# A fused attention and expert block: start of the attention reordered, expert stage begun inside the attention's end

## The reference

```python
mod = (silu(c) @ wmod).reshape(4, 6, 1, 256)
sa, ca, ga, sb, cb, gb = (mod[:, n] for n in range(6))
ga, gb = (2 * (g >= 0) - 1) * max(abs(g), 0.25)      # for both
h = layernorm(x) * (1 + ca) + sa
x = x + ga * attention(h)      # 16 heads of 128, scores masked, softmax, W_O
h = layernorm(x) * (1 + cb) + sb
x = x + gb * ffn(h)
```

## Time and profile before

| what | us |
|---|---|
| median of three runs | 830.65 (829.01 to 832.02) |
| the profiled execution, its own time | 829.57 |
| its span, first to last instruction | 827.8 |
| TensorE busy | 796.7 (96%) |
| VectorE busy | 675.7 (82%) |
| ScalarE busy | 629.1 (76%) |
| POOL busy | 448.9 (54%) |
| mean granted clock of TensorE | 0.988 of 2.4 GHz |

### The profile page before, as it was taken

The page is one execution under the profiler, slowest core; times in us unless marked ns, Lnnn a source line. Parts: engine busy times, 40 slices in busy tenths (PEclk is TensorE's granted clock), DMA queues, the critical chain, the costliest instruction groups (busy, mean ns, idle before and its releaser), DMA issues.

```text
span 827.8 us, 14504 instructions
## 1 busy us (share of the span) xinstructions
PE 796.7 (96%) x4832; PEld 708.6 (86%) x4832; DVE 675.7 (82%) x1636; ACT 629.1 (76%) x1408; POOL 448.9 (54%) x310
## 2 busy tenths in 40 slices
...
DMA packets 47593, 70.54 MB, mean 85 GB/s; under 512 B 5536, under 2 KB 38464, under 8 KB 47392
## 3 DMA queue, kind: packets, MB, share of 16 engines
...
q10 hardware_dynamic: 144, 0.00, 0.0%
HBM read 25.49 MB, written 2.17 MB: 33 GB/s over the span
## 4 chain that ended last, share of the span: by engine, by line
PE 74%; ACT 11%; DVE 8%; issue 3%; POOL 2%; DMA 1%; SPq 0%; DVEq 0%; POOLq 0%; ACTq 0%
PE M L712 15%; PE M L713 15%; PE M L711 15%; PE S L711 6%; PE S L713 6%; PE S L712 6%; ACT PB L610 3%; PE T L711 2%; PE T L713 2%; PE T L712 2%; ACT PB L657 2%; DVE S L1098 2%; ACT qk L670 1%; ACT pth L681 1%; DVE gab L1114 1%
## 5 line engine op out<-in xcount | busy, mean ns | idle before, releaser
L610 ACT ACTIVATE PB<-S,nb 128x128 f32<-128x128 f32 (+3 forms) x256 | 133.8, 533 | 111.6 <-DVE nb L1098 111.6
L567 POOL TENSOR_TENSOR ptl<-ptl,pth 128x640 fp32r<-128x640 f32 x128 | 198.9, 1577 | 35.1 <-ACT pth L681 35.1
L560 POOL TENSOR_TENSOR X<-X,fb 128x512 f32<-128x512 f32 x64 | 83.2, 1301 | 245.5 <-DVE fb L1127 245.5
L1087 DVE TENSOR_TENSOR qk<-M,qk 128x512 fp32r<-128x512 f32 x128 | 88.4, 690 | 52.9 <-ACT qk L670 52.9
L657 ACT ACTIVATE PB<-PB,ri 128x256 f32<-128x256 f32 (+3 forms) x256 | 124.4, 580 | 5.4 <-DVE ri L1107 5.2
L1098 DVE CUSTOM_DVE_ANT_0 S<-S,cc 128x128 f32<-128x128 f32 (+3 forms) x256 | 117.6, 523 | 1.3 <-PE S L713 1.3
L1114 DVE STREAM_TRANSPOSE gab<-PB 128x256 f32<-128x256 f32 (+2 forms) x192 | 109.3, 623 | 0.3 <-DMA ptl<-gab 0.3
L711 PE MATMUL M<-hh,W 128*128 128x512 f32 x264 | 103.9, 394 | 1.2 <-DVE hl L1073 0.9
L712 PE MATMUL M<-hl,W 128*128 128x512 f32 x264 | 103.3, 391 | 0.0
L713 PE MATMUL M<-hh,W 128*128 128x512 f32 x264 | 103.2, 391 | 0.0
L681 ACT CAST pth<-ptl 128x640 fp32r<-128x640 f32 x128 | 87.6, 742 | 3.5 <-DMA ptl<-gab 3.5
...
## 6 DMA issues: line engine op xcount, KB each, us to landing
ptl<-gab SPq DMA_DIRECT2D x256, 160.0 KB, 3.1
stage<-in_wat SPq DMA_DIRECT2D x16, 512.0 KB, 5.0
...
X<-in_x SPq DMA_DIRECT2D x3, 512.0 KB, 7.9
stage<-in_wfa SPq DMA_DIRECT2D x3, 512.0 KB, 4.7
out<-X SPq DMA_DIRECT2D x3, 512.0 KB, 2.6
...
```

The lines of the kernel that those rows point to most:

```text
L560: pool.tensor_tensor(X[:, a:a + 512], X[:, a:a + 512], fb[:, c2 * 512:c2 * 512 + 512], ALU.add).then_inc(s_y, 1)
L567: pool.tensor_tensor(ptl[u % 2][:, s], ptl[u % 2][:, s].bitcast(F32), pth[u % 2][:, s].bitcast(F32), ALU.subtract).then_inc(s_pl, 1)
L610: ins = act.activation(PB[:, P_OFF[i]:P_OFF[i] + w], PS[bk][:, a:a + w], ACT.Exp, bias=nb[:, i:i + 1], scale=-1.0, accum_out=sm[:, i:i + 1])
L1087: v.tensor_tensor(lo, src, hi.bitcast(F32), ALU.subtract).then_inc(me, 1)
```

## The change

In the start: the four small loads of POOL (`bcol`, `b2`, `ub`, `cb`) are issued behind the second piece of weights (`wh(1)`) and not at once; the warming matmuls behind `mod` go from 16 to none, those behind `h(0,1)` from 12 to 8; the second scaling of `h(0,0)` is done by VectorE into a score bank; `mg`'s matmul goes ahead of S(0), its evacuation on VectorE becomes a step `mv` behind S(0), and batch 1's statistics follow it; POOL's part stays at `mg`; `pt(0)` and `mh` (load of ga) go ahead of `norm(1)`; `ms` goes ahead of `tr(1)`; `wh(3)` and `ld(5)` go behind unit 1.

In the attention's end: the loop ends two units earlier, and z(62), z(63), the last `wo`, `pt(63)`, r(1), the statistics of batch 2's second LayerNorm, rs(0,12..14) and `wt(0)` are placed by hand, from `w1(0)` on among the experts' chunks. For it the attention's buffers are laid out anew (P of even units beside PB), pieces 20 and 21 of the weights only wait for the last q and k, and the first GELU waits for the last `ty`. The experts run in the order 3, 2, 1, 0, 4, 5, 6, 7 (the weights are stored in that order). `wt(1)` is one chunk later.

```diff
-EXPERT = [e for e, h in enumerate(HID) for _ in range(h // 128)]
+ORDER = [3, 2, 1, 0, 4, 5, 6, 7]
+PLACE = [n for n, e in enumerate(ORDER) for _ in range(HID[e] // 128)]
 LAG = 3
 EULER = 2.718281828459045
-WARM = 60, 16, 12
+WARM = 60, 0, 8
...
-    put(post, 0, ("ms",))
...
-        put(post, 57 + 4 * b, ("r", b))
+    put(post, 57, ("r", 0))
     fill[58] = [[("rs", 0, 1), ("rs", 0, 2)]] + fill[58]
     put(post, 58, *[("rp", 0, c) for c in range(4)])
     fill[59] += [[], [("rs", 0, 3)], [("rs", 0, 4)]]
     fill[60] = [[("rs", 0, k)] for k in range(5, 10)]
-    fill[61] = [[("rs", 0, k)] for k in range(10, 15)]
-    put(post, 61, ("wt", 0))
-    fill[62] = [[("st", 6, 0), ("st", 6, 1)], [("st", 6, 2)], [("st", 6, 3)], [("nm", 6, 0), ("nm", 6, 1)]]
-    put(post, 61, ("wh", 20), ("ld", 22))
+    fill[61] = [[("rs", 0, 10)], [("rs", 0, 11)]]
+    put(post, 60, ("wh", 20))
     plan = [("mod0",)] + [("st", 0, k) for k in range(4)] + [
         ("silu",), ("nb", 0), ("nm", 0, 0), ("nm", 0, 1), ("mod",), ("wh", 0), ("ld", 2),
         ("h", 0, 0), ("h", 0, 1), ("wh", 1), ("ld", 3),
-        ("q", 0), ("st", 1, 0), ("st", 1, 1), ("k", 0), ("wh", 2), ("ld", 4), ("S", 0), ("st", 1, 2), ("st", 1, 3),
-        ("q", 1), ("ri", 0), ("k", 1), ("norm", 0), ("nb", 1), ("ty", 0), ("nm", 1, 0), ("nm", 1, 1), ("v", 0, 0),
-        ("mg",), ("tr", 0), ("S", 1), ("q", 2), ("ri", 1), ("k", 2), ("norm", 1), ("ty", 1), ("pt", 0), ("mh",), ("v", 0, 1),
-        ("wh", 3), ("tr", 1)]
-    loads = {0: [5]}
+        ("q", 0), ("k", 0), ("wh", 2), ("ld", 4), ("mg",), ("S", 0), ("mv",), ("st", 1, 0), ("st", 1, 1),
+        ("ri", 0), ("q", 1), ("st", 1, 2), ("st", 1, 3), ("k", 1), ("norm", 0), ("nb", 1), ("ty", 0),
+        ("nm", 1, 0), ("nm", 1, 1), ("v", 0, 0), ("tr", 0),
+        ("S", 1), ("q", 2), ("ri", 1), ("k", 2), ("pt", 0), ("mh",), ("norm", 1), ("ty", 1), ("v", 0, 1), ("ms",),
+        ("tr", 1)]
+    put(post, 1, ("wh", 3), ("ld", 5))
+    loads = {}
...
-    for i in range(NU):
+    for i in range(NU - 2):
...
-        if i + 2 == NU:
-            plan += [("dn", 0), ("b1",)]
-    return plan
+    last = NU // 2 - 2
+    plan += [("dn", 0), ("b1",), ("wo", last, 0), ("wo", last, 1), ("z", NU - 2), ("wh", 21), ("ld", 22)]
+    return plan + [("rs", 0, k) for k in range(12, 15)]
...
-    put(0, 0, ("wh", 21))
-    put(0, 0, ("rs", 1, 1))
-    put(0, 1, ("rs", 1, 2), ("wo", last, 0))
-    put(0, 2, ("wo", last, 1), ("wl", 0), ("wl", 1))
-    put(0, 3, ("wh", 22))
-    for k in range(3):
-        put(0, 2 + k, ("d0", k))
-    put(0, 4, ("h2", 2, 0))
-    put(0, 5, ("h2", 2, 1), ("wl", 2), ("wl", 3))
-    for k, j in enumerate((6, 7, 8, 9)):
+    put(0, 0, ("pt", NU - 1))
+    put(0, 1, ("r", 1), ("st", 6, 0), ("st", 6, 1))
+    put(0, 2, ("wt", 0), ("wl", 0), ("st", 6, 2), ("st", 6, 3))
+    put(0, 3, ("wh", 22), ("rs", 1, 1), ("rs", 1, 2))
+    put(0, 4, ("z", NU - 1), ("nm", 6, 0), ("nm", 6, 1))
+    put(0, 5, ("h2", 2, 0), ("d0", 0))
+    put(0, 6, ("wo", last, 0), ("h2", 2, 1), ("d0", 1))
+    put(0, 7, ("wo", last, 1), ("wl", 1), ("wl", 2), ("wl", 3), ("d0", 2))
+    for k, j in enumerate((9, 10, 11, 11)):
         put(0, j, ("st", 7, k))
     for c in range(3):
         put(0, 9 + c, ("dta", c))
-    put(0, 12, ("dt",), ("nm", 7, 0))
-    put(0, 14, ("nm", 7, 1))
+    put(0, 12, ("dt",))
+    put(0, 13, ("nm", 7, 0))
+    put(0, 15, ("nm", 7, 1))
...
-        at_(n + 17 - (b == 1), ("wt", b))
+        at_(n + 17, ("wt", b))
...
+            pt0 = sa("pth0", 1280, F32R), sa("ptl0", 1280, F32R)
             vh, vl = sa("vh", 2048, F32R), sa("vl", 2048, F32R)
-            pth = [sa("pth0", 1280, F32R), sa("pth1", 1280, F32R)]
-            ptl = [sa("ptl0", 1280, F32R), sa("ptl1", 1280, F32R)]
+            pt1 = sa("pth1", 1280, F32R), sa("ptl1", 1280, F32R)
+            pth, ptl = [pt0[0], pt1[0]], [pt0[1], pt1[1]]
             zt = sa("zt", 2048, F32R)
         ur = sb("ur", 2048, F32R)
         Gr = sb("Gr", 4096, F32R)
+        gob = sb("gob", 256)
+        ol, oh = sb("ol", 512, F32R), sb("oh", 512, F32R)
+        sb("gap", 512)
+        prod = sb("prod", 1024)
         gxh, gxl = sb("gxh", 2048, F32R), sb("gxl", 2048, F32R)
-        oh, ol = sb("oh", 512, F32R), sb("ol", 512, F32R)
-        prod = sb("prod", 1024)
-        gob = sb("gob", 256)
...
-            return ("v", NU // 2 - 1, 1)
+            return (("q", NU - 1), ("k", NU - 1), ("v", NU // 2 - 1, 1))[n - 20]
...
-                        sp.wait_ge(me, use[("wo", NU // 2 - 1, 1)] + 1)
+                        sp.wait_ge(me, use[("wo", NU // 2 - 5 + 4 * i, 1)] + 1)
                     elif i < 4:
                         sp.wait_ge(mf, use[("h2", 2, 1)] + 1)
                     else:
                         sp.wait_ge(s_ac, acc_no[divmod(i - 4, 8)[0], (i - 4) % 8 + 1] + 1)
-                    sp.dma_start(wb_at(i), scw[i:i + 1, :].broadcast_to([128, 512])).then_inc(s_wb[i % 4], 16)
+                    row = i // 8 * 8 + ORDER[i % 8]
+                    sp.dma_start(wb_at(i), scw[row:row + 1, :].broadcast_to([128, 512])).then_inc(s_wb[i % 4], 16)
...
-            pool.dma_start(bc[:], bcol).then_inc(s_bc, 16)
-            pool.dma_start(rows[:, 0:128], b2).then_inc(s_b, 16)
-            pool.dma_start(oub[:], ub.broadcast_to([128, 256])).then_inc(s_b, 16)
-            pool.dma_start(gab[:, 0:256], cb.broadcast_to([128, 256])).then_inc(s_b, 16)
...
+                    pool.dma_start(bc[:], bcol).then_inc(s_bc, 16)
+                    pool.dma_start(rows[:, 0:128], b2).then_inc(s_b, 16)
+                    pool.dma_start(oub[:], ub.broadcast_to([128, 256])).then_inc(s_b, 16)
+                    pool.dma_start(gab[:, 0:256], cb.broadcast_to([128, 256])).then_inc(s_b, 16)
...
-                    act.activation(bank(ev)[:], bank(ev)[:], ACT.Identity, bias=bias, scale=scale).then_inc(s_v, 1)
+                    if ev != ("h", 0, 0):
+                        act.activation(bank(ev)[:], bank(ev)[:], ACT.Identity, bias=bias, scale=scale).then_inc(s_v, 1)
...
+                    if n == 0:
+                        act.wait_ge(s_ty, NU)
...
-                elif kind == "mg":
+                elif kind == "mv":
                     v.wait_ge(s_b, 48)
                     v.wait_ge(s_bc, 16)
                     v.tensor_tensor(oub[:], oub[:], gab[:, 0:256], ALU.add).then_inc(s_ob, 1)
                     v.tensor_scalar(bc[:, B_SH2:B_SH2 + 1], bc[:, B_SH2:B_SH2 + 1], 0.1, None, ALU.mult).then_inc(s_ob, 1)
-                    v.wait_ge(mf, use[ev] + 1)
-                    v.tensor_copy(rows[0:4, 640:1152], bank(ev)[0:4, :]).then_inc(me, 1)
+                    v.wait_ge(mf, use[("mg",)] + 1)
+                    v.tensor_copy(rows[0:4, 640:1152], bank(("mg",))[0:4, :]).then_inc(me, 1)
...
+                    if ev == ("h", 0, 0):
+                        v.wait_ge(mh, rd[ev] + 1)
+                        v.wait_ge(s_mc, 1)
+                        link(v.tensor_scalar(PS[1][:], bank(ev)[:], modt[:, 8:9], modt[:, 0:1], ALU.mult, ALU.add))
+                        v.tensor_tensor(lo, PS[1][:], hi.bitcast(F32), ALU.subtract).then_inc(me, 1)
+                        continue
...
```

More of the change, by code:

```diff
@@ L204, in EXP_OF @@
     t, j = divmod(n, NC + 1)
-    return t, (0 if j == 0 else 1 + EXPERT[j - 1])
+    return t, (0 if j == 0 else 1 + PLACE[j - 1])
 MISC = {"h": True, "q": True, "k": True, "v": True, "z": True, "wo": False, "h2": True, "r": False,
```

10 lines of the change are left out of this document (5 added, 5 removed).

## The result

The changed kernel takes 842.3 us (median of 4 runs, 838.58 to 844.14) against 830.12 (4 runs, 829.01 to 832.02) for the kernel before on the same chip: ratio 1.0131, 95% interval 1.0097 to 1.0164. It is slower, by more than the range of the prediction holds.

What follows compares the result with a forecast made beforehand. TensorE was taken to bound 140 to 560 us and VectorE 60 to 140, leaving the attention's two ends to win. Start +4.3, end +0.3, experts -1.4 gave +3.2 and 833.5 us; range 826 to 837.5.

Steps and rivals of the forecast that it cites:

- After that the work to w2(5) is 8.3 us: End of attention, behind the stall at h2(2,0): w2(5) ends at 673.1, or 674.8 with low clock; before, 674.35.
- -1.4: Expert stage: wt(1), which waited 2.17, moves one chunk of 1.4 us later and gains 1.4 (0 to 2.2).
- Each later tile has the same work: Expert stage: no gain or loss was added for the later tiles.
- Start, +4.3: Start of the kernel: gains less delays leave it 4.3 us slower, bounds 2.5 to 5.8.
- POOL's chain ahead of the power: Start: POOL's 8.2 us of gate work precedes batch 1's LayerNorm power, so ty(0) begins at 33.35, 5.3 later.
- The 0.8 for the small loads: Start: issuing the four small loads later lets the modulation's weights land 0.8 us earlier, bounds 0 to 1.5.
- The end, +0.3: Attention's end: the 7.1 us wait at wt(0) becomes a 4.8 stall at h2(2,0); net +0.3, bounds -1.2 to +1.5.
- Rival (d), the clock: Fewer warming matmuls and new idle time lengthen the 1.2 GHz stretches: +3.4 us, 837.3; chance 0.10.
- (a): Attention's end: VectorE keeps up, nm(6) is done when TensorE reaches h2(2,0), saving 7.0 us: 826.9; chance 0.18.
- (b): Start: POOL's chain hides and ty(0) isn't held, so the start is -1.2: 828.4; chance 0.13.
- (c): Both ends: VectorE keeps up at the end and POOL's chain hides at the start: 821.4; chance 0.11.
- The signs: Trace times and waits named beforehand, from POOL's first gate operation near 24 us to wt(1)'s wait of about 0.8.

Runs made afterwards that it cites:

- e7: Changed kernel with the old start, e4's router, and st(6), nm(6), rs(0,12..14), d0 ahead of z(62): 827.5 us, ratio 0.996 to the kernel before.
- e4: Changed kernel with router steps rs(b,3) to rs(b,9) one chunk later: 840.5 us, ratio 1.0129 to the kernel before.
- e11: e7 with the new start order, POOL's gate work behind the power, norm(1) before pt(0), wh(21) behind w1(1), d0 behind h2(2,0): 827.1 us.
- e16: e7 with wh(21) behind w1(1), late small loads, fewer warming matmuls, h(0,0) scaled on VectorE, d0 at chunks 3 to 5, nm(7) at 12, 14: 824.7 us.
- e1: Changed kernel with POOL's gate work at v(0,0), behind the LayerNorm power of batch 1: 836.6 us, ratio 1.0082 to the kernel before.
- e5: e1 with pt(0) and mh again behind norm(1) and ty(1): 838.7 us, ratio 1.0097 to the kernel before.
- e2: Changed kernel with wh(3) and ld(5) again ahead of tr(1): 845.6 us, ratio 1.0177 to the kernel before.

## Why the prediction was wrong

It said +3.2 us and 833.5; it was +12.3 in the profile. The direction that was called likeliest of the three (slower) was right, the size was not.

- **The step that failed is that the sum was closed at w2(5), with nothing for the order of the work behind it.** "After that the work to w2(5) is 8.3 us" was compared with the earlier trace rows, and all behind it was "**-1.4**" for `wt(1)` and "Each later tile has the same work". Measured from `w1(9)` on: +8.6. Of this, 1.1 is `d0(2)`, late for the 16-column matmuls (e7 without it: 0), and 3.1 the low clock there, whose cause stays open. 2.5 is lost between `w1(13)` and `w1(17)`, in the product's wait at 697.64 (0.66) and the wait for `nm(7)` at `h2(3,0)` (1.70). Of this, 0.6 goes with e4's router steps (1.9 lost in each of e4 and e7 to e11), and 1.9 with `nm(7)` and `d0` moved forward (e16: both waits gone). The last 1.9 is the router in tiles 1 and 2 (e4). The work is the same in each tile; its order among POOL's steps isn't. And `wt(1)` gave 0.1, not 1.4: its 2.17 went, but `w1(22)` now waits 1.65 for its S bank (712.79), a wait that had stood hidden behind the other.
- **Start, +4.3, was +7.2.** POOL's chain ahead of the power was right in place and nearly in size (`ty(0)` at 33.65 for 33.35, S(1)'s masks at 36.95 for 36.85), and e1 takes 5.2 back. That the times agree so closely is partly luck: S(0) was 0.8 later than worked out, and the chain from it to `ty(0)` 0.5 shorter (13.5 for 14). `pt(0)` ahead of `norm(1)`, put at 2.0: 1.8 by the trace of e5. The miss of 2.9 is about the sum of three things: the small loads' 0.8 (below), 1.0 for "The last piece of W (`wh 3`) and its load move to ScalarE and POOL gaps: nothing", and some 1.1 for the low clock behind the wait for it (e2). The prediction named the gaps and didn't check when `wo(0,0)` wants the piece. The 7.2 is of one execution; the seven others with this start stand at 7.0 to 10.7 at unit 6.
- **The 0.8 for the small loads was 0.** The modulation's matmuls began at 8.27, before at 8.24; over all profiles at 8.05 to 8.79 with the loads first and at 7.81 to 9.22 with them behind. S(0) came 1.7 earlier all the same, which is the rest of that sum to the tenth, and it counted in full, as all behind it keeps its distance from S(0) (above).
- **The end, +0.3, was -3.35.** z(62) ended at 655.5, 648.3 without the start's 7.2, as worked out, and the idle 2.8 ahead of `wo(30,0)` was 2.67 (649.35). The stall did go to `h2(2,0)`, with 2.49 for 4.8: TensorE came to it 0.5 later than worked out, and `nm(6)` was through 1.9 earlier (670.05; 662.9 without the start). I had summed durations of 0.68, but such operations start 0.60 apart. The gain up to w2(5) was larger for it, and also because the 1.6 that the sum kept for the low clock there did not come in this execution. (e1, with the same end, did have it: a low stretch at 665 to 668, and 24.1 us from `w1(0)` to `w1(9)` for 22.7.)
- **Rival (d), the clock, at 0.10** with +3.4, was the nearest. It was right in kind: the low clock behind `w1(9)` cost 3.1 (up to 6.2 in other profiles), and one in the start some 1.1. But it is a third of the 12.3. (a), (b) and (c) are out: `h2(2,0)` waits, and `ty(0)` was held.
- **The signs.** POOL's gate work at 24.39, the power at 32.48, `ty(0)` after 32, S(3) on TensorE at 57.05 (55 to 57 was named) and `wt(0)`'s wait of 1.23 came as named. The wait at `h2(2,0)` was under its 3 to 6, and the one at `wt(1)` was gone where 0.8 was named. All of them lie ahead of the place where most was lost.
